# Causal relative attention in a four-sublayer kernel: relative products written unit by unit, selects in place of mask products

## The reference

```
q, k, v = projections (16 heads of width 16), 4 batches: 64 heads
QEr  = einsum('bhsd,ld->bhsl', q, Er)          # [512 rows, 512 positions] per head
Srel = _skew(QEr)                              # pad one column in front, reshape: row s, column t reads QEr[s, 511 - s + t]
attn = (einsum('bhsd,bhtd->bhst', q, k) + Srel) / 4
attn = where(causal, attn, -inf);  out = softmax(attn) @ v
```

## Time and profile before

| | |
|---|---|
| median of 3 runs | 1244.4 us |
| profiled execution | 1246.87 us, its span 1245.1 us |
| mean granted TensorE clock | 0.923 of full speed |
| PE, VectorE, ScalarE, GpSimd busy | 85%, 53%, 51%, 16% of the span |
| causal attention (first product at 56.4 us, last at about 400 us) | some 344 us |

### The profile page before, as it was taken

One profiled execution on the slowest core, in us unless ns is written; L12 is line 12 of the kernel. 1 busy time (PEld: TensorE's weight loads), 2 busy tenths in 40 slices (PEclk: granted clock), 3 DMA queues, 4 the chain that ended last, 5 costly groups with the idle time before them and its releaser, 6 DMA issues. The chain is left out here.

```text
span 1245.1 us, 21943 instructions
## 1 busy us (share of the span) xinstructions
PE 1055.8 (85%) x6945; PEld 658.0 (53%) x6979; DVE 660.2 (53%) x1993; ACT 633.1 (51%) x1245; POOL 199.1 (16%) x466
## 2 busy tenths in 40 slices
PE   7879998887897769899999994537999999987487
PEld 4436554544554549899899993212333333334244
DVE  4416877676685651121111110866766666684697
ACT  2437766666662323233222231425777777763787
POOL 0000000000000011232222220002222222230232
PEclk9957999899899979899999997768999999998799
DMA  5087888888884934676666662463111111100001
GB/s 177 1 285 267 288 269 273 267 264 260 260 262 163 350 137 135 237 223 216 224 228 213 213 213 87 155 195 115 46 45 45 50 45 44 48 29 9 0 31 38
DMA packets 75342, 199.55 MB, mean 160 GB/s; under 512 B 7880, under 2 KB 40904, under 8 KB 69256
## 3 DMA queue, kind: packets, MB, share of 16 engines
q1 hardware_dynamic: 71528, 188.45, 46.6%
q0 software_dynamic: 3744, 10.23, 2.1%
HBM read 134.82 MB, written 63.83 MB: 160 GB/s over the span
## 5 line engine op out<-in xcount | busy, mean ns | idle before, releaser
L765 DVE CUSTOM_DVE_ANT_0 unused<-mpsS,mask_bias 128x512 bf16<-128x512 f32 x256 | 172.0, 691 | 82.7 <-PE mpsS L698 82.3
L1506 ACT ACTIVATE hT<-ph,w 128x128 f32<-128x128 f32 x312 | 89.0, 368 | 206.6 <-PE ph L1480 206.6
L792 ACT ACTIVATE mPT<-mpsB 128x512 f32<-128x512 f32 x256 | 152.6, 597 | 80.8 <-PE mpsB L705 67.1
L1480 PE MATMUL ph<-xT,w 128*128 128x128 f32 x1248 | 151.1, 281 | 7.4 <-DMA w<-in_w1p 6.2
L1480 PEld LDWEIGHTS ph<-xT,w 128*128 128x128 f32 x1248 | 146.6, 196 | 10.2 <-issue 10.0
L1525 DVE TENSOR_TENSOR xn<-py,b 128x256 f32<-128x256 f32 x39 | 16.6, 425 | 246.6 <-PE py L1490 246.6
L1490 PE MATMUL py<-w,hT 128*128 x624 | 141.2, 379 | 0.7 <-DVE xn L1525 0.7
L633 ACT COPY stage<-psE 128x1024 f32<-128x1024 f32 (+1 forms) x96 | 83.1, 865 | 112.1 <-DMA rel<-stage 61.9
L640 ACT ACTIVATE scores<-scores,nm 128x512 f32<-128x512 f32 (+3 forms) x256 | 125.4, 555 | 9.2 <-DVE nm L608 9.2
L1490 PEld LDWEIGHTS py<-w,hT 128*128 128x128 f32 x624 | 115.6, 190 | 15.2 <-issue 1.1
L595 DVE CUSTOM_DVE_ANT_0 scores<-psS,bias 128x512 f32<-128x512 f32 (+3 forms) x176 | 77.9, 488 | 84.7 <-PE psS L538 82.5
(11 more groups left out here) (251 smaller groups left out, 1594.4 us busy)
## 6 DMA issues: line engine op xcount, KB each, us to landing
rel<-stage SPq DMA_DIRECT2D x64, 640.0 KB, 7.9
w<-in_w1p SPq DMA_DIRECT2D x39, 1028.0 KB, 5.8
bias<-rel SPq DMA_DIRECT2D x44, 640.0 KB, 4.6
x<-rel SPq DMA_DIRECT2D x20, 640.0 KB, 5.7
mqk<-packed SPq DMA_DIRECT2D x64, 192.0 KB
w<-in_w2p SPq DMA_DIRECT2D x8, 1024.0 KB, 12.9
b<-in_b SPq DMA_DIRECT2D x39, 128.0 KB, 6.0
got<-pair_out SPq DMA_DIRECT2D x8, 512.0 KB, 8.7
```

The costliest lines, as they stand in the source:

```text
L765: nc.vector.tensor_tensor_reduce(out=unused[:, i, :], in0=psS[i % 2][:, :], in1=mask_bias[:, i, :], scale=1.0, scalar=-3.0e38, op0=ALU.add ...
L792: nc.scalar.activation(PT[r][:, j, :], psB[j % 2][:, :], ACT.Exp, scale=1.0 / 4).then_inc(s_exp, 1)
L1480: mm = nc.tensor.matmul(ph[half][:, q * P:(q + 1) * P], w1[i][:, dk * F + f * P:dk * F + (f + 1) * P], xT[i][:, dk, :], start=(dk == 0), s ...
L1506: g = nc.scalar.activation(hT[i][:, f, :], ph[half][:, q * P:(q + 1) * P], ACT.Gelu, bias=w1[i][:, DK * F + f:DK * F + f + 1])
```

## The change

Four things are changed, all in the causal attention.

1. **The mask.** `hide` is gone. GpSimd runs four `affine_select` per pair on the stage, one for each block (both heads at once, 2 x 128 columns): in the first 128 columns of a block's part it keeps those from 127 - r on in row r and fills the others with -2^100. These are columns that the block's own skewed rows never use, while the skewed rows of the block in front of it run into them with just the part above the diagonal. After the last block stands one more column of -2^100 (`REL_P` = 1281).
2. **The writes.** A pair has one HBM buffer for both heads (128 x 2 x 1281, ring of four), and SP writes it in three DMAs, one per unit, each as soon as the selects of that unit are done: 256 rows of 512, 512 and 257 elements. ScalarE waits for the landing of a unit's own write of pair p-2.
3. **SP's order** in a step is now write(n+5, unit 0), read(n+4), write(n+5, unit 1), write(n+5, unit 2).
4. **The first three pairs** put their units' relative products in `psE`, `psS` and `psT`, which are not yet in use then.

```diff
+    REL_P = REL_W + 1
-    rel = [dram(f"rel_{r}", (P, REL_W), F32) for r in range(ROUND)]
+    rel = [dram(f"rel_{r}", (P, 2, REL_P), F32) for r in range(RING)]
...
+                def relative_bank(p, u):
+                    return (psE, psS, psT)[u] if p < REL - SOFT else psE
...
                     def read(p):
+                        for u in range(NU):
+                            sp.wait_ge(s_wr[p % RING][u], 16 * (p // RING + 1))
                         for h in range(2):
-                            slot = (2 * p + h) % ROUND
-                            sp.wait_ge(s_wr[slot], 16 * (2 * p // ROUND + 1))
...
-                            skewed = bass.AP(rel[slot].ap().tensor, P - 1, [[REL_W - 1, P], [1, REL_W]])
+                            skewed = bass.AP(rel[p % RING].ap().tensor, P - 1 + h * REL_P, [[2 * REL_P - 1, P], [1, REL_W]])
...
-                    def write(p):
-                        sp.wait_ge(s_eev, NU * (p + 1))
-                        for h in range(2):
...
-                            sp.dma_start(rel[slot][:, :], stage[p % 2][:, h, :]).then_inc(s_wr[slot], 16)
+                    def write(p, u):
+                        cols = slice(512 * u, 512 * u + WU[u] if u < NU - 1 else REL_P)
+                        sp.wait_ge(s_cut, 4 * p + (1, 3, 4)[u])
...
+                        sp.dma_start(rel[p % RING][:, :, cols], stage[p % 2][:, :, cols]).then_inc(s_wr[p % RING][u], 16)
...
-                        if (p := pair_at(n, READ)) is not None:
-                            read(p)
-                        if (p := pair_at(n, REL)) is not None:
-                            write(p)
+                        early, back = pair_at(n, REL), pair_at(n, READ)
+                        if early is not None:
+                            write(early, 0)
+                        if back is not None:
+                            read(back)
+                        if early is not None:
+                            write(early, 1)
+                            write(early, 2)
...
                     def relative(p, u):
-                        wait(pe, s_eev, NU * p + u)
+                        wait(pe, s_eev, NU * (p - 1) + u + 1 if p < REL - SOFT else NU * p + u)
...
-                    def hide(p, u):
...
+                    for i in range(2):
+                        nc.vector.memset(stage[i][:, :, REL_W:], NEG).then_inc(s_edge, 1)
...
                 def _(pool):
-                    pool.wait_ge(vals.s_zero, 3)
-                    for g in range(NBH // GROUP):
-                        vals.spread_values(pool, g, g % 2)
+                    keep = dict(base=-(P - 1), channel_multiplier=1, compare_op=ALU.is_ge, fill=nc.gpsimd.to_reg(NEG))
+                    for n in range(-REL, NP):
...
+                        if n >= 0 and n % 2 == 0:
+                            vals.spread_values(pool, n // 2, n // 2 % 2)
+                        if (p := pair_at(n, REL)) is not None:
+                            for u, unit in enumerate(units):
+                                pool.wait_ge(s_eev, NU * p + u + 1)
+                                pool.sem_inc(s_seen_pool, 1)
+                                for i, off, w in unit:
+                                    first = stage[p % 2][:, :, 512 * u + off:512 * u + off + P]
+                                    nc.gpsimd.affine_select(out=first, in_=first, pattern=[[0, 2], [1, P]], **keep).then_inc(s_cut, 1)
...
-                        if early is not None and early >= 2:
-                            for h in range(2):
-                                m = 2 * (early - 2) + h
-                                act.wait_ge(s_wr[m % ROUND], 16 * (m // ROUND + 1))
...
+                                if early >= 2:
+                                    act.wait_ge(s_wr[(early - 2) % RING][u], 16 * ((early - 2) // RING + 1))
```

More of the change, by code:

```diff
@@ L442, in causal_attention @@
             with ExitStack() as ctx:
-                stage = [sb(ctx, f"stage{r}", [P, 2, REL_W]) for r in range(2)]
+                stage = [sb(ctx, f"stage{r}", [P, 2, REL_P]) for r in range(2)]
                 bias = [sb(ctx, f"bias{r}", [P, 2, REL_W]) for r in range(2)]
@@ L453, in causal_attention @@
                 psT = ctx.enter_context(nc.psum_tensor("psT", [P, 2, 512], F32))
-                s_wr = [sem(f"s_wr{r}") for r in range(ROUND)]
+                s_wr = [[sem(f"s_wr{r}_{u}") for u in range(NU)] for r in range(RING)]
                 s_rd = [sem(f"s_rd{r}") for r in range(ROUND)]
                 s_back = sem("s_back")
-                names = ("emm", "eev", "smm", "soft", "nm", "exp", "tmm", "tev", "seen", "seensp")
-                s_emm, s_eev, s_smm, s_soft, s_nm, s_exp, s_tmm, s_tev, s_seen, s_seen_sp = (
+                names = ("emm", "eev", "smm", "soft", "nm", "exp", "tmm", "tev", "seen", "seensp", "cut", "edge", "seenpool")
+                s_emm, s_eev, s_smm, s_soft, s_nm, s_exp, s_tmm, s_tev, s_seen, s_seen_sp, s_cut, s_edge, s_seen_pool = (
                     sem(f"s_{n}") for n in names)
@@ new lines, in read @@
+                            sp.dma_start(bias[p % len(bias)][:, h, :], skewed).then_inc(s_rd[(2 * p + h) % ROUND], 16)
+                    def write(p, u):
+                        cols = slice(512 * u, 512 * u + WU[u] if u < NU - 1 else REL_P)
+                        sp.wait_ge(s_cut, 4 * p + (1, 3, 4)[u])
+                        if p == 0 and u == 0:
+                            sp.wait_ge(s_edge, 2)
+                        if p >= RING:
+                            for h in range(2):
+                                m = 2 * (p - RING) + h
+                                sp.wait_ge(s_rd[m % ROUND], 16 * (m // ROUND + 1))
+                        sp.dma_start(rel[p % RING][:, :, cols], stage[p % 2][:, :, cols]).then_inc(s_wr[p % RING][u], 16)
@@ L523, in relative @@
                             for i, off, w in units[u]:
-                                mm = nc.tensor.matmul(psE[:, h, off:off + w], query(p, h, i), er[rows, S - w:S],
+                                mm = nc.tensor.matmul(relative_bank(p, u)[:, h, off:off + w], query(p, h, i), er[rows, S - w:S],
                                                       start=True, stop=True)
@@ L528, in score @@
                     def score(p, u):
+                        if p == 0 and u == 0:
+                            pe.wait_ge(s_eev, NU * (REL - SOFT - 1) + 2)
                         for h in range(2):
                             wait(pe, s_soft, piece(p, u, h) - 1)
-                            for at, (i, off, w) in enumerate(units[u]):
-                                nc.tensor.matmul(psS[:, h, off:off + w], query(p, h, i), key(p, h, w),
-                                                 start=(at == 0), stop=False)
-                    def hide(p, u):
-                        for h in range(2):
-                            for at, (i, off, w) in enumerate(units[u]):
-                                mm = nc.tensor.matmul(psS[:, h, off + w - P:off + w], identb[:, :], dmask[:, :],
-                                                      start=False, stop=(at == len(units[u]) - 1))
+                            for i, off, w in units[u]:
+                                mm = nc.tensor.matmul(psS[:, h, off:off + w], query(p, h, i), key(p, h, w),
+                                                      start=True, stop=True)
                             mm.then_inc(s_smm, 1)
@@ L545, in turn_probs @@
                                 pe.wait_ge(s_exp, 2 * p + h + 1)
+                            if p == 0 and u == 0 and h == 0:
+                                pe.wait_ge(s_eev, NU * (REL - SOFT))
                             if h == 0:
@@ L631, in _ @@
                             if early is not None:
+                                if early >= 2:
+                                    act.wait_ge(s_wr[(early - 2) % RING][u], 16 * ((early - 2) // RING + 1))
                                 act.wait_ge(s_emm, NU * early + u + 1)
                                 nc.scalar.copy(stage[early % 2][:, :, 512 * u:512 * u + WU[u]],
-                                               psE[:, :, 0:WU[u]]).then_inc(s_eev, 1)
+                                               relative_bank(early, u)[:, :, 0:WU[u]]).then_inc(s_eev, 1)
                             if soft is None:
```

9 lines of the change are left out of this document (3 added, 6 removed).

## The result

The changed kernel takes 1237.1 us (median of 11 runs, 1230.24 to 1242.51) against 1247.75 for the kernel before in the same series (11 runs, 1243.69 to 1252.51): ratio **0.9915**, 95% interval 0.9891 to 0.9939, some 10.6 us less. Forecast were 31 us less. The profiled execution took 1238.75 us, its span 1237.0, granted clock 0.910.

A forecast was written before the change was run, and what follows sets the result against it. It took PE and ScalarE turns, then PE, then from pair 12 the relay through HBM to bound the causal attention. Start -8, mask products -2.4 and HBM loop -20.5 gave -31 us: 1213 us, range 1190 to 1244.

The forecast's parts named there:

- What bounds it: Causal attention: PE and ScalarE alternating in first pairs, PE in pairs 3 to 12, the HBM relay in 12 to 31.
- The start: Pairs 0 to 2: with a pair of banks for each unit PE need not wait between units; -8 us.
- The HBM loop: Pairs 6 to 31: the step falls from a mean of 9.52 us to 8.7; -20.5 us over 25 pairs.
- The second read need not wait for a landing of its own any more: HBM loop: of the 1.2 us wait between a pair's two reads, 0.3 us was counted as saved.
- the write in the hole: HBM loop: the first unit's write, put before the reads, fills the DMA engines' idle time; 1.4 us a pair saved.
- the short writes: HBM loop: packets of 2 KB and 1 KB in place of 5 KB make a pair's writes 0.4 us longer.
- The mask products: PE, eight fewer a pair: 0.5 us at full clock, 0.8 at half; -2.4 us in three pairs after the start.
- Selects, SP, code loading: Additions in the causal attention cost nothing: selects of 0.5 us, five SP DMAs a pair, no GpSimd loading seen.
- the loop keeps its length: Rival: reads still wait for the third write, 9.94 us for all 25 pairs, 1244 us; chance 0.14.
- Engines bind: Rival: the HBM loop is cut until it vanishes, 7.9 us a pair, 1193 us; chance 0.17.
- Slow writes: Rival: writes off 256 B boundaries fall to the reads' rate, 5.6 us, loop 10.7 a pair, 1263 us; chance 0.10.
- The clock: Rival: the fuller start returns full clock earlier, from pair 3 on or never falling, 1205 to 1209 us; chance 0.04.

The follow-up runs named there:

- e1: Kernel before, with SP reading a pair's skewed rows one step later; 1213.67 us, ratio 0.9739 to the kernel before.
- e3: Kernel before, with only the separate bank pairs for the first three pairs added; ratio 1.0004 to the kernel before.
- e9: Kernel before, with one HBM buffer, one write and one landing for both heads of a pair; 1266.06 us, ratio 1.0164.
- e10: Changed kernel, with a buffer, a write and a read for each head again; ratio 1.0078 to the kernel before.
- e7: Changed kernel, with one write a pair after all selects in place of three; 1271.17 us, ratio 1.0195 to the kernel before.
- e11: Changed kernel, with the first unit's write put behind the reads in SP's queue; 1279.04 us, ratio 1.0285 to the kernel before.
- e6: Changed kernel, with one write a pair in place of three and the reads one step later; 1201.16 us, ratio 0.9631 to the kernel before.
- e2: Changed kernel, with the reads one step later; 1222.72 us, ratio 0.9802 to the kernel before.
- e5: Kernel before, with separate bank pairs for the first three pairs and the reads one step later; 1204.18 us, ratio 0.9664.

## Why the prediction was wrong

The sign was right, the size was not. By its own steps:

- **What bounds it**: right. The relay was the pace of pairs 12 to 31 (e1).
- **The start** (-8): the part itself gave -13.4, more than forecast. Pair 1 took 3.4 us at half clock where 5.4 was counted: without waits the products of different units overlap, and 5.4 was the time with waits between them. But the sum added this lead to the rest, and it never reached the relay, whose first read is issued at 67.06 us against 66.80. From there on the relay is the pace, and e3 shows the same in the kernel before. The prediction had itself said that the lead is used up by pair 12, and then counted a new lead as time.
- **The HBM loop** (-20.5, a step of 8.7): **this is the step that failed**, in one term: "The second read need not wait for a landing of its own any more ... and I count 0.3 of it". That wait was not a cost but the stagger of two heads. Giving it up costs 0.68 us where 0.3 was credited (e9; 0.41 between e10 and e7). The other two terms of the step were nearly right: the write in the hole gave 1.3 us, not 1.4 (e11), and the short writes cost 0.15 to 0.4, not 0.4 (e7, e11). The runs form a chain, 9.94, 10.63 with one landing and the selects (e7), 10.78 with three writes (e11), 9.48 with the first one moved; that its links add up is no test of them.
- The step was then set against 9.52, the mean with the six pairs that lived on the old lead. Like for like, 25 pairs at 9.39 save 3.3 us.
- **The mask products**: about 0.2 us a pair rather than 0.5 where PE is the pace. In pairs 3 to 6, where they were to give 2.4 us, nothing is gained (+1.8): ScalarE waits 4.47 us for a landing in pair 3, and SP's reads come every 9.2 to 9.9 us there too, with PE at half clock close behind. Why the time from start to start of a group was too much is not shown.
- **Selects, SP, code loading**: the selects took 408 ns, and e7 with them and e9 without them have the same step, 10.63 and 10.62. What is left open is e10's 0.28.
- **The rivals**: nearest came *the loop keeps its length*. One of its reasons, that the last unit's write gates the reads, is what SP's waits show; but what was gained in front was lost to the single landing, not to short packets and selects. *Engines bind* is what happens once the reads go later (e6, 7.96 to 8.05 a pair where 7.9 was priced). *Slow writes*: no, 3.5 us as priced; but the three short writes do fill the DMA engines, which only shows in e2.
- **The clock**: full clock didn't come from pair 3 on. From 80 to 110 us the mean was 0.57 against 0.52, and in the middle there was more half clock (0.91 against 0.97). It isn't the pace: between 100 and 345 us SP's reads come every 9.48 us on average in the five steps with much half clock, and every 9.44 in the other twenty, while a pair's copies come 7.7 to 13.5 us after the last pair's.
- Behind the causal attention nothing changed, as forecast: 844.5 and 843.7 us.

## What to carry to other kernels

Where a stage is a relay (write, landing, read, next write), its step is the sum of the pieces in the loop, and the cheapest cure is to take the landing out of it by issuing the read one step later, if its consumer has the slack: one constant gave more than the whole change. Before two transfers are merged, look whether the wait between them is an overlap. A gain at the front of a relay counts only if the relay isn't the pace behind it.

## What the runs showed of the hardware

- A read phase behind a hole is slow: 1.31 MB in about 5 us. In e7 it moves 257 GB/s although the DMA engines are busy for 0.93 of it; the same reads, with writes queued around them, go at a mixed rate of 320 GB/s at a share of 0.88 (e1). A relay loses more than its hole.
- From SP's issue of a read to its first data 0.9 us pass when nothing is in flight (e7).
- The granted clock was 2.4 GHz for all of 110 to 330 us in e1 and e5, where PE is busy for 97% of it. In the kernels with a closed relay it fell to 1.2 GHz for parts of it (means of 0.84 to 0.97). The order isn't that of PE's busy share: e10, busy for 78%, has 0.94, and the changed kernel, busy for 93%, has 0.91. Here half clock cost little, because the relay was slower still.
